# Routed experts in five full-height down products, and the shared output as a fifth combine term

## Time and profile before

| | |
|---|---|
| median of 3 runs | 727.38 us (724.78 to 810.8) |
| the profiled execution | 726.9 us |
| its span, first to last instruction | 725.1 us |
| mean granted TensorE clock | 0.868 |
| PE, DVE, ACT, POOL busy | 73%, 61%, 47%, 48% |
| routed loop f = 0, about | 92 to 266 us |
| routed loop f = 1, about | 457 to 631 us |
| combine after f = 1, about | 636 us to the end |

### The profile page before, as it was taken

One profiled execution on the slowest core, in us unless ns is written; L12 is line 12 of the kernel. 1 busy time (PEld: TensorE's weight loads), 2 busy tenths in 40 slices (PEclk: granted clock), 3 DMA queues, 4 the chain that ended last, 5 costly groups with the idle time before them and its releaser, 6 DMA issues.

```text
span 725.1 us, 14307 instructions
## 1 busy us (share of the span) xinstructions
PE 528.3 (73%) x3442; PEld 488.8 (67%) x3443; DVE 440.1 (61%) x1253; ACT 341.3 (47%) x1001; POOL 344.6 (48%) x355
## 2 busy tenths in 40 slices
PE   4887489999999970586667896799999999800000
PEld 3765389999999970365547674699999999700000
DVE  5486547777777753567844686377777777513233
ACT  3568445555555540365564465355555555400000
POOL 2379544444444407777404022544444444067774
PEclk9989879999999995788898989799999999955555
DMA  8950224443434423333202300234343435234443
GB/s 263 298 166 31 66 79 123 126 123 123 123 123 123 122 73 101 102 101 98 64 0 99 108 31 10 81 123 125 121 125 120 128 121 121 80 99 125 130 132 99
DMA packets 51577, 79.92 MB, mean 110 GB/s; under 512 B 8485, under 2 KB 37541, under 8 KB 51549
## 3 DMA queue, kind: packets, MB, share of 16 engines
q0 software_dynamic: 13824, 37.77, 19.3%
q1 hardware_dynamic: 37725, 41.82, 17.6%
HBM read 52.29 MB, written 27.26 MB: 110 GB/s over the span
## 4 chain that ended last, share of the span: by engine, by line
PE 55%; POOL 20%; issue 12%; DMA 4%; ACT 4%; DVE 3%; SPq 0%; POOLq 0%; DVEq 0%; ACTq 0%
PE bank L925 40%; POOL mamba_room L370 17%; PE bank L947 5%; PE bank L981 5%; DMA xn_scratch<-ring_f 3%; POOL ring_f L360 2%; PE bank L1025 2%; ACT ring_f L487 2%; DMA ys_scratch<-ring_f 1%; PE bank L1012 1%; ACT w_routed L406 1%; PE bank L1027 1%; PE bank L990 1%; ACT xres L474 1%; PE bank L1052 1%
## 5 line engine op out<-in xcount | busy, mean ns | idle before, releaser
L925 PE MATMUL bank<-w_routed,ring_r 128*128 (+1 forms) x1920 | 314.7, 313 | 2.8 <-DVE ring_r L647 1.6
L925 PEld LDWEIGHTS bank<-w_routed,ring_r 128*128 128x128 f32 (+1 forms) x1920 | 282.7, 191 | 4.6 <-issue 4.5
L360 POOL DMA_INDIRECT ring_f<-xn_scratch,tokidx x160 | 155.4, 972 | 207.7 <-PE bank L947 176.8
L370 POOL DMA_INDIRECT mamba_room<-ys_scratch,si x128 | 126.6, 989 | 74.5 <-issue 38.4
L790 DVE SCALAR_TENSOR_TENSOR xres<-mamba_room,wk,xres 128x256 f32<-128x256 f32 (+1 forms) x128 | 53.4, 478 | 97.2 <-DMA mamba_room<-ys_scratch,si 97.2
L663 DVE TENSOR_TENSOR ring_f<-bank,ring_f 128x176 f32<-128x176 f32 x160 | 54.5, 341 | 57.7 <-ACT ring_f L441 57.6
L441 ACT ACTIVATE ring_f<-bank 128x176 f32<-128x176 f32 x160 | 50.8, 317 | 81.5 <-PE bank L925 81.5
L655 DVE TENSOR_TENSOR ring_r<-bank,ring_r 88x256 fp32r<-88x256 f32 x160 | 67.3, 421 | 33.3 <-ACT ring_r L433 28.7
L447 ACT ACTIVATE ring_f<-ring_f 128x176 f32<-128x176 f32 x160 | 56.1, 351 | 65.4 <-DVE ring_f L663 65.4
L647 DVE TENSOR_TENSOR ring_r<-bank,ring_r 128x256 fp32r<-128x256 f32 x160 | 66.0, 413 | 17.1 <-ACT ring_r L425 17.1
L673 DVE COPY ring_f<-bank 128x256 f32<-128x256 f32 x160 | 67.8, 424 | 13.2 <-DMA ys_scratch<-ring_f 2.3
(11 more groups left out here) (118 smaller groups left out, 562.6 us busy)
## 6 DMA issues: line engine op xcount, KB each, us to landing
ys_scratch<-ring_f SPq DMA_DIRECT2D x160, 128.0 KB, 1.7
raw_routed<-in_w13r SPq DMA_DIRECT2D x6, 704.0 KB
xn_scratch<-ring_f SPq DMA_DIRECT2D x32, 128.0 KB, 2.3
raw_routed<-in_w13r SPq DMA_DIRECT2D x8, 352.0 KB
ring_f<-xn_scratch,tokidx POOLq DMA_INDIRECT x160
raw_routed<-in_w2r SPq DMA_DIRECT2D x6, 352.0 KB
xres<-in_x_in SPq DMA_DIRECT2D x4, 512.0 KB, 5.9
mamba_room<-ys_scratch,si POOLq DMA_INDIRECT x128, 2.8
```

Of the source, the lines that this page charges most:

```text
L360: pool.indirect_dma_start(xg[j % UN], None, xn_dram, bass.IndirectOffsetOnAxis(ap=tokidx[:, j:j + 1], axis=0)).then_inc(s_g[j % UN], 16)
L370: pool.indirect_dma_start(cg[t % 4][:, q, :], None, ys_dram, bass.IndirectOffsetOnAxis(ap=si[:, n:n + 1], axis=0)).then_inc(s_cg[t % 4], 16)
L925: last = pe.matmul(out, a, b, start=(q == 0), stop=(q == len(terms) - 1))
```

## The change

**Down products.** The inner width is cut in 128 + 48. The hidden tile is 256 columns: 176 real ones, 16 zeros, the last 48 again, 16 zeros. Transposed, the second half has the 48 in rows 0 to 47 and again in rows 64 to 111. Its high part keeps the first copy high, and DVE puts the low part in place of the second; the w2 rows are stored twice in the same way. So high x high and low x high of these 48 are one product, and the six products become five. The w2 room of an expert has 128 rows in place of 88, with more bytes to load.

**Queues of the loop.** The copy of the result moves from DVE to ACT (`act_slot_out`). The DVE's hidden product and hidden low are two instructions each. ACT and DVE take the hidden stages one step later and in another order. Lags of PE are as before.

**Shared output.** The product with 2 x identity is gone. `evict` writes to one of two buffers, SP writes that to DRAM (`shared_out`), and `evict` waits for the write of two tiles earlier. In the combine SP reads it back (`shared_in`) and DVE adds it as a fifth term.

**Picks and weight copies.** Three pick buffers. The highs of experts 0 to 3 move from ACT to DVE among tiles 7 to 10; ACT's other highs are packed into shared steps 2 to 6, and only expert 15's stays among the picks. POOL makes expert 15's low before the gathers. A count product reads its operand without stride, four multiplications are one, two casts are gone, four short memsets are new.

```diff
-DVE_UP = (0, 1, 2, 13, 14, 15)
+NHD = 4
+DVE_UP = (0, 1, 2, 3, 15)
 POOL_UP = tuple(e for e in range(NE) if e not in DVE_UP)
 SH_ENDS, SH_ALL = 10, NT + 1
+CHAIN_HIGHS = {2: (7, 8), 3: (9, 10), 4: (11, 12), 5: (13,), 6: (14,)}
+TERMS = TOPK + 1
...
-        hid = [ring_f[:, 1024 + b * H:1024 + (b + 1) * H] for b in range(2)]
-        yb = [ring_f[:, 1376 + b * D:1376 + (b + 1) * D] for b in range(2)]
+        hid = [ring_f[:, 1024 + b * 2 * P:1024 + (b + 1) * 2 * P] for b in range(2)]
+        up = [stage[1][:, 512 + b * H:512 + (b + 1) * H] for b in range(2)]
+        yb = [ring_f[:, 1536 + b * D:1536 + (b + 1) * D] for b in range(2)]
...
+            def shared_out(f, t):
+                sp.wait_ge(s_yo, f * STEPS + t + 1)
+                sp.dma_start(sh_dram[t * P:(t + 1) * P, :], sh_out[t % 2]).then_inc(s_sw[t % 2], 16)
+
+            def shared_in(f, t):
+                if t >= 4:
+                    sp.wait_ge(s_cd, term(f, t - 4, TERMS - 1))
+                sp.dma_start(cg[t % 4][:, TOPK, :], sh_dram[t * P:(t + 1) * P, :]).then_inc(s_cs[t % 4], 16)
...
+                for t in range(6):
+                    shared_out(f, t)
...
                 sp.wait_ge(s_ht, f * STEPS + 8)
                 load_late(NE - 1)
+                for t in range(6, NT):
+                    shared_out(f, t)
...
-                for e in range(0 if f == 0 else MAMBA_E, NE - 1):
-                    low_expert(e, e + 1 + f * (NE - MAMBA_E))
+                for e in range(0 if f == 0 else MAMBA_E, NE):
+                    low_expert(f, e)
                 pool.wait_ge(s_rt, f + 1)
                 for k in range(UN):
                     pool.wait_ge(s_xw[k], 16 * (NT // UN) * (f + 1))
-                for j in range(UN):
-                    gather(f, j)
-                low_expert(NE - 1, NE + f * (NE - MAMBA_E))
-                for j in range(UN, NS):
+                for j in range(NS):
                     gather(f, j)
                 for b in range(2):
...
-                    act.activation(hT[b][0][0:HC, :], p_hT[b][0:HC, 0:2 * P], ACT.Copy).then_inc(s_hhi, 1)
+                    act.activation(hT[b][0], p_hT[b][:, 0:2 * P], ACT.Copy).then_inc(s_hhi, 1)
...
+                    act.activation(up[b], p_h[b][:, H:2 * H], ACT.Copy).then_inc(s_a, 1)
+                return stage
+
+            def act_slot_out(f, base):
+                def stage(i, c):
+                    b = c % 2
+                    act.wait_ge(s_y, base + i * UN + c + 1)
+                    if not (isinstance(i, int) and i * UN + c < 2):
+
+                        act.wait_ge(s_yw[b], 16 * (f * (NS // 2) + i * (UN // 2) + c // 2))
+                    act.activation(yb[b], p_y[b][:, 0:D], ACT.Copy).then_inc(s_yo, 1)
...
-                    act.activation(hid[c % 2], hid[c % 2], ACT.Silu).then_inc(s_s, 1)
+                    act.activation(hid[c % 2][:, 0:HD + HB], hid[c % 2][:, 0:HD + HB], ACT.Silu).then_inc(s_s, 1)
...
-                act.activation(xres[:, t, :], p_yS[t % 2][:, 0:D], ACT.Copy, scale=0.5).then_inc(s_yo, 1)
+                if t >= 2:
+                    act.wait_ge(s_sw[t % 2], 16 * (f * (NT // 2) + t // 2))
+                act.activation(sh_out[t % 2], p_yS[t % 2][:, 0:D], ACT.Copy, scale=0.5).then_inc(s_yo, 1)
...
-                        high_expert(f, n + 1)
+                        for e in CHAIN_HIGHS.get(n, ()):
+                            high_expert(f, e)
...
-                    if f == 0 and t % 3 == 1 and t < 12:
-                        high_expert(f, SH_ENDS + 1 + t // 3)
-                    if t == 13:
+                    if t == 11:
...
-                pipeline(act, NS, [(LAG_X, act_x(base)), (LAG_H, act_first(base)),
-                                   (LAG_H, act_silu(base)), (LAG_T, act_ht(base))])
+                for b in range(2):
+                    act.wait_ge(s_sw[b], 16 * (NT // 2) * (f + 1))
+                pipeline(act, NS, [(LAG_H + 1, act_first(base)), (LAG_T + 1, act_ht(base)), (LAG_X, act_x(base)),
+                                   (LAG_H + 1, act_silu(base)), (LAG_Y + 1, act_slot_out(f, base))])
...
-                    dve.tensor_tensor(hT[b][1][0:HC, :], p_hT[b][0:HC, 0:2 * P], hT[b][0][0:HC, :].bitcast(f32),
-                                      ALU.subtract).then_inc(s_hlo, 1)
+                    dve.tensor_tensor(hT[b][1][:, 0:P], p_hT[b][:, 0:P], hT[b][0][:, 0:P].bitcast(f32), ALU.subtract)
+                    rest = hT[b][0][64:P, P:2 * P]
+                    dve.tensor_tensor(rest, p_hT[b][64:P, P:2 * P], rest.bitcast(f32), ALU.subtract).then_inc(s_hlo, 1)
...
-                    dve.tensor_tensor(hid[b], p_h[b][:, 0:H], hid[b], ALU.mult).then_inc(s_m, 1)
...
+                    dve.tensor_tensor(hid[b][:, HD:HD + HB], p_h[b][:, P:H], up[b][:, P:H], ALU.mult)
+                    dve.tensor_tensor(hid[b][:, 0:H], p_h[b][:, 0:H], up[b], ALU.mult).then_inc(s_m, 1)
...
+            def high_expert(e):
+
+                dve.wait_ge(s_we[e // 2], 32)
+                dve.tensor_copy(w_routed[:, e, 0, 0:W13], raw_routed[e // 2][:, e % 2, 1, 0:W13])
+                dve.tensor_copy(w_routed[:, e, 0, W13:WE], raw_routed[e // 2][:, e % 2, 1, W13:WE]
+                                ).then_inc(s_whd, 1)
...
-                for k in range(TOPK):
-                    last = dve.tensor_tensor(prod[:, :, k, :], oh[:, :, k, :], sl, ALU.mult)
-                link(last)
+                link(dve.tensor_tensor(prod, oh, sl.unsqueeze(2).broadcast_to((P, NT, TOPK, NE)), ALU.mult))
...
+                for b in range(2):
+                    dve.memset(hid[b][:, H:HD], 0.0)
+                    dve.memset(hid[b][:, HD + HB:2 * P], 0.0)
...
+                            dve.tensor_tensor(xr, xr, cg[2 * c + b][:, q, :], ALU.add).then_inc(s_cd, 1)
...
-                    if f == 0 and t in (12, 14):
-                        low_up(t // 2 - 6, t // 2 - 5)
+                    if f == 0 and 7 <= t < 7 + NHD:
+                        high_expert(t - 7)
+                    if f == 0 and 7 + NHD <= t < 7 + 2 * NHD:
+                        low_up(f, t - 7 - NHD)
...
-                pipeline(dve, NS, [(LAG_X, dve_x(base)), (LAG_H, dve_product(base)),
-                                   (LAG_Y, dve_slot_out(f, base)), (LAG_T, dve_ht(f))])
+                for b in range(2):
+                    dve.wait_ge(s_sw[b], 16 * (NT // 2) * (f + 1))
+                pipeline(dve, NS, [(LAG_H + 1, dve_product(base)), (LAG_T + 1, dve_ht(f)), (LAG_X, dve_x(base))])
...
-                    mm3(p_y[b][:, 0:D], [(hT[b][0][0:HC, q * P:(q + 1) * P], hT[b][1][0:HC, q * P:(q + 1) * P],
-                                          w(HC, 0, W13 + q * D, D), w(HC, 1, W13 + q * D, D)) for q in range(2)]
-                        ).then_inc(s_y, 1)
+                    hi, lo = hT[b]
+                    for q, (a, v) in enumerate([(hi[:, 0:P], w(P, 0, W13, D)),
+                                                (lo[:, 0:P], w(P, 0, W13, D)),
+                                                (hi[:, 0:P], w(P, 1, W13, D)),
+                                                (hi[:, P:2 * P], w(P, 0, W13 + D, D)),
+                                                (hi[:, P:2 * P], w(P, 1, W13 + D, D))]):
+                        last = pe.matmul(p_y[b][:, 0:D], a, v, start=(q == 0), stop=(q == 4))
+                    last.then_inc(s_y, 1)
...
-                    for q in range(2):
-                        last = pe.transpose(p_hT[b][0:HC, q * P:(q + 1) * P], hid[b][:, q * HC:(q + 1) * HC], ident)
-                    last.then_inc(s_ht, 1)
+                    pe.transpose(p_hT[b][:, 0:P], hid[b][:, 0:P], ident)
+                    pe.transpose(p_hT[b][:, P:2 * P], hid[b][:, P:2 * P], ident
+                                 ).then_inc(s_ht, 1)
...
-                    pe.matmul(p_yS[t % 2][:, 0:D], hTs[t % 3][0:HC, q * P:(q + 1) * P], w2_shared[:, q * D:(q + 1) * D],
-                              start=(q == 0), stop=False)
-                pe.matmul(p_yS[t % 2][:, 0:D], twice, xres[:, t, :], start=False, stop=True).then_inc(s_y, 1)
+                    last = pe.matmul(p_yS[t % 2][:, 0:D], hTs[t % 3][0:HC, q * P:(q + 1) * P],
+                                     w2_shared[:, q * D:(q + 1) * D], start=(q == 0), stop=(q == 1))
+                last.then_inc(s_y, 1)
...
-                    last = pe.matmul(p_tot, hcst[:, H_ONE:H_ONE + P], oh[:, :, k, :].rearrange("p t e -> p e t"),
+                    last = pe.matmul(p_tot.rearrange("p (e t) -> p t e", e=NE), hcst[:, H_ONE:H_ONE + P], oh[:, :, k, :],
...
+    w2r = np.zeros((NE, P, 2, D), np.float32)
+    w2r[:, :, 0] = a["L0_ffn_w2_routed"][:, 0:P]
+    w2r[:, 0:HB, 1] = w2r[:, 64:64 + HB, 1] = a["L0_ffn_w2_routed"][:, P:H]
+    w2r = w2r.reshape(NE, P, W2C)
```

130 lines of the change are left out of this document (68 added, 62 removed).

## The result

The changed kernel takes 695.47 us (median of 4 runs, 694.2 to 697.2) against 727.18 us of the kernel before beside it: a ratio of 0.9576, with a 95% interval from 0.9541 to 0.9611. The profiled execution took 695.84 us, with a span of 693.6; 693 was predicted.

The account below looks back on a forecast made before the run. PE was taken to bound the routed loop, POOL's pace the combines, and no engine was full in the pick stages. 726.9 - 18.9 - 8.0 - 4.8 - 4.0 + 1.6 = 692.8, so 693 us; range 683 to 706, some 0.82.

Parts of the forecast that it names:

- Down products: Routed loop: one product of 0.118 us less per slot tile, 160 times, -18.9 us; bounds 0 and 19.
- Start of the loops: Start of each routed loop: expert 15's low made ahead of the gathers lets PE start 4.0 us earlier per ffn, -8.0.
- First ffn: First ffn up to the end of its picks: picks run from 61 to 78.3 us in place of 83.1, -4.8.
- the rival of writes behind the loads: First ffn: shared writes wait behind weight loads, picks come 5 to 10 us later, 698 to 703 us; chance 0.20.
- The count product: Routing ahead of the picks: the count product drops from 1.88 us to the 0.61 of its neighbour, -1.3.
- Second picks: Second ffn: picks take 17.3 us in place of 19.3 and start 2.0 earlier, -4.0.
- Combines: End of either combine: only the last pair's two extra additions of 0.42 us show, +0.8 twice; bounds 0.5 and 3.
- POOL's gathers are untouched: Combines: the step claiming that the shared output's fifth term leaves POOL's gathers as they were, within the +0.8 each.
- the gap after each gather: Last combine: POOL works 62.4 of 89 us, and the rest of its time was said to be this gap.
- Loop unchanged: Routed loop: the product goes, but PE waits for ACT's or DVE's longer lists, 712 us; chance 0.07.
- ACT-bound: Routed loop: ACT becomes the bound with a step of 2.55 us, 778 us, slower than before; chance 0.04.
- the first, second and last: Whole kernel: as summed, 687 to 700, 0.62; writes behind the loads, 698 to 703, 0.20; better, about 685, 0.07.

Follow-up runs that it names:

- old_orders: The changed kernel with the routed loop's ACT and DVE orders of the kernel before, the result's copy staying on ACT: 1.0548 of the kernel before, 790.9 us.
- before_low_front: The kernel before with one edit, POOL making the down low of expert 15 ahead of the first four gathers: 0.9886 of the kernel before, 744.1 us.

## Why the prediction came out, point by point

- **Down products, -18.9: right.** Measured alone 19.4. A product of 128 rows costs 0.121 us where one of 88 rows cost 0.118, and ACT and DVE keep up, but only in the new orders (66 us hang on them).
- **Start of the loops, -8.0: right in cause, the size known to 2 us.** The low alone is worth 6.0 taken back out of the changed kernel, and 8.6 put into the kernel before. In the changed kernel PE's first transposes are not the whole loop: the second tile's gather then sets the pace for a step. The loop stages gained 29.6 in all, not 26.9, by a term that I didn't have: the first gather's 3.13 us was DVE's three lows beside it. It is 1.6 us shorter per ffn; 19.4 + 6.0 + 3.0 = 28.4 of the 29.6, or 31.0 with the 8.6.
- **First ffn, -4.8: 1.4 too small.** The sigmoid comes 0.7 us later (38.0, now 38.7), not 2.3: the loads move at 310 GB/s where the earlier trace rows had 281, and DVE's highs fill its idle time. The first scaling starts at 58.8, not 61; the evictions wait for their writes for 0.3 us in all, so the rival of writes behind the loads didn't happen. The row of all 32 evictions, with what their engine waited for:

```profile
  PE bank L1079: 4.4, 2
  DMA shared_scratch<-ring_f: 0.3, 1
```

- **The count product, -1.3: wrong.** I had taken the 1.88 us of the second product, less the 0.61 of its neighbour, for the price of its access form. With the operand read without stride it takes 1.91, and its neighbour 1.03:

```profile
45.37 1.03 PE L1092 MATMUL bank<-ring_f,hcst 128*128 128x256 f16 x4 [0.99 <-DVE ring_f L755]
...
46.20 1.91 PE L1094 MATMUL bank<-ring_f,hcst 128*128 128x256 f16 x4
```

  The table by stages for these 2 us, first of the kernel before, then of the changed one, has part of the cause in the figure behind the five engines:

```profile
45.00:47.00 2.00, 2.00 (x9) 0.79 (x7) 0.32 (x2) 0.40 (x1) 1.52 (x2) 0.60 0.72 219
```

```profile
45.00:47.00 2.00, 1.63 (x7) 0.99 (x8) 0.93 (x4) 2.00 (x5) 2.00 (x2) 0.50 0.22 77
```

  The granted clock is 0.50, the lower level of 1.2 GHz; in the kernel before it was 1.00 until 45, while the first product ran, and 0.60 in these 2 us. In either kernel PE had waited 1.0 to 1.2 us for DVE's membership just ahead. In the second ffn of the kernel before, both at the lower level, the same two took 1.04 and 1.91 us. So the two rows were not to be compared: the clock makes the 0.61 a 1.03. The other 0.9 us, which the second product takes more than its neighbour at one and the same clock, are there with the old form and with the new one. The edit had taken the stride from the operand that is read and given it to the result that is written (`p_tot.rearrange`), so no run here has this product without one.
- **Second picks, -4.0: 1.4 too large.** The first scaling comes 2.1 us earlier from the norms, as predicted (2.0), though not by the 1.3 of the count product that stood in it: the two products take 1.04 and 1.91 there before and after. So this match is luck. And the stage takes 18.8 and not 17.3: DVE's picks start 1.00 apart only where no shared step lies between, 17.6 us from first to last and not 15.
- **Combines, +0.8 each: the failed term.** The last one is right on the first chip (+0.5). The first one costs 6.4. "POOL's gathers are untouched" was the step that failed: their instructions were, but DVE's additions lengthen the run of DVE instructions with two operands in SBUF that holds a gather of most pairs, from 1.28 to 1.95 us. The rows that could have told it were there: gathers of 1.28 us at the end of DVE's sums, and the 3.13 us beside the lows. That POOL's other time in the last combine is "the gap after each gather" is right for 19.2 of the 26.6 us only; the rest lies behind the last gather.
- **Rivals.** Loop unchanged, ACT-bound and late writes did not happen, and old_orders shows the second to be real one edit away. The chance of 0.88 for a faster kernel was too small for its own cases: the first, second and last alone make 0.89. The sum of 693 was met by luck, since +5.6 stood against -2.7 and smaller ones; it was better than its terms.

Open: the 1.1 us behind the last gather of the first combine; which part of a gather's issue DVE holds (it ends 1.02 or 0.87 us after DVE's run at the start of a loop, 0.82 after it in a combine, and some pass within a run of sums); what the second count product would take without a stride; and why the gathered rows land later on the other chips.

## What to carry to other kernels

A gather issued by POOL has a price that DVE sets: look for gathers that are longer than their neighbours and read which DVE run with two operands in SBUF ends some 0.8 to 1.0 us ahead of their end, before moving DVE work next to them. What ends together with them need not be the cause: the statistics did, and hold nothing. A term that is ready early belongs at the head of a sum, where the engine waits anyhow. And when a product is taken off a full engine, the orders of the engines around it are part of the price: with a step of lag more they cost nothing, without it they cost three times what the product gives.

## What the hardware showed that was not expected

- A gather's issue went from 0.95 us to 1.28, 1.40, 1.53, 1.95 and 3.13 us beside unbroken DVE instructions with two float32 operands in SBUF, whatever their form: lows, plain additions, products with sums. Beside statistics alone, with one operand in SBUF, it stayed at 0.95.
- The same four fp16 count products took 0.61 us at a granted clock of 1.00 and 1.03 at 0.50, and those with a stride in operand or result 1.91 at 0.50; 128-row and 88-row products with 256 moving columns at full clock start 0.12 us apart alike.
- ACT's instructions of 0.36 to 0.41 us follow each other every 0.26 to 0.31 us, DVE's of 0.42 every 0.34, so their sums overstate what a step needs by up to a third.
- The kernel before took 727 us on one chip and 750 on two that are taken to be others. Its loops, seen in before_low_front, have the same length there; the difference lies in the combines, where DVE's sums start up to 9 us behind the gathers and not 3.
